# A two-layer graph and expert kernel: four up units move ahead of the routing's transposes, the routing weights of the first chunk travel alone, and two normalisations begin chunk by chunk

## What is computed

```
x = x + gnn0(layernorm(x), adj)    # attention over adj, then two GRU cells
x = x + ffn0(layernorm(x))         # one shared + 8 routed experts, hidden 512, gelu
x = x + gnn1(layernorm(x), adj)    # relu(adj @ (bilinear features) + ...)
x = x + ffn1(layernorm(x))         # 8 routed experts, hidden 256, relu

# both ffn: logits = h @ Wr (+ bias); the two largest of 8 get softmax weights, the rest 0
# out = sum over experts e of weight[:, e] * (act(h @ W1[e] + b1[e]) @ W2[e] + b2[e])
```

## Time and profile before

| | |
|---|---|
| time, three runs | 2235.76 us median (2234.46 to 2236.96) |
| time of the profiled execution | 2233.43 us, span 2231.6 us |
| busy: PE, DVE, ACT, POOL | 1819.9, 1693.7, 1398.4, 188.7 us |
| mean granted clock of PE | 0.904 of full speed |
| GRU part, its last PE work ends | 1180.0 us |
| first normalisation | 1191.9 to 1221.4 us |
| expert stage 0, from the router to the last expert | 1220.1 to 1626.9 us |
| third normalisation | 1970.1 to 1999.7 us |
| expert stage 1 | 1998.4 us to the end |

### The profile page before, as it was taken

One profiled execution on the slowest core, in us unless ns is written; L12 is line 12 of the kernel. 1 busy time (PEld: TensorE's weight loads), 2 busy tenths in 40 slices (PEclk: granted clock), 3 DMA queues, 4 the chain that ended last, 5 costly groups with the idle time before them and its releaser, 6 DMA issues.

```text
span 2231.6 us, 30437 instructions
## 1 busy us (share of the span) xinstructions
PE 1819.9 (82%) x8958; PEld 871.5 (39%) x9101; DVE 1693.7 (76%) x1792; ACT 1398.4 (63%) x1767; POOL 188.7 (8%) x154
## 2 busy tenths in 40 slices
PE   4221573899999999999797799999986699986997
PEld 4111221344444444444345344444452244462332
DVE  4555327788898888889466788888859988846998
ACT  1676006788788788788234567676645577625886
POOL 0000001100000000000442000000017700000000
PEclk7555788899999999999897899999979999977999
DMA  5997025555555554554500311221030089713542
GB/s 160 430 427 312 0 79 209 166 153 160 157 153 156 166 153 149 169 154 155 208 0 0 78 38 38 60 54 38 1 133 0 0 348 428 314 38 78 96 92 76
DMA packets 79540, 313.86 MB, mean 141 GB/s; under 512 B 13942, under 2 KB 14422, under 8 KB 69462
## 3 DMA queue, kind: packets, MB, share of 16 engines
q1 hardware_dynamic: 79468, 312.98, 41.7%
HBM read 297.88 MB, written 15.08 MB: 140 GB/s over the span
## 4 chain that ended last, share of the span: by engine, by line
PE 40%; DVE 10%; POOL 3%; issue 3%; ACT 1%; DMA 1%; DVEq 0%; SPq 0%; POOLq 0%; ACTq 0%; another core or an unknown queue 0%
PE psum L925 8%; PE psum L915 8%; PE psum L988 7%; PE psum L859 7%; POOL halves L484 3%; DVE hidp L1363 2%; DVE xT L1385 2%; DVE yT L1382 2%; DVE prod L1422 2%; PE psum L883 1%; PE psum L885 1%; PE psum L726 1%; PE psum L731 1%; PE psum L897 1%; PE psum L737 1%
## 5 line engine op out<-in xcount | busy, mean ns | idle before, releaser
L586 ACT ACTIVATE ss<-KR,dpt 128x1024 bf16<-128x1024 int16 x384 | 413.1, 1138 | 112.0 <-DVE pl L1255 111.3
L859 PE MATMUL psum<-ph,Tt 128*128 128x512 bf16 x1502 | 412.2, 381 | 8.8 <-DVE pl L1255 7.0
L669 ACT ACTIVATE hid<-psum,fB 128x512 f32<-128x512 f32 x416 | 270.7, 686 | 143.7 <-PE psum L915 89.0
L925 PE MATMUL psum<-hidp,fW 128*128 128x512 bf16 x1218 | 291.7, 381 | 28.6 <-DVE hidp L1363 22.6
L915 PE MATMUL psum<-hTp,fW 128*128 (+1 forms) x1229 | 291.3, 381 | 4.5 <-ACT mk L654 3.2
L1363 DVE TENSOR_TENSOR hidp<-hid,hidp 128x512 bf16<-128x512 f32 x416 | 268.7, 687 | 25.9 <-DVE xT L1385 10.1
L1252 DVE TENSOR_TENSOR ph<-ss,Ahi 128x3072 bf16<-128x3072 bf16 x128 | 225.2, 1759 | 62.0 <-PE psum L859 60.3
L859 PE MATMUL psum<-pl,Tt 128*128 128x512 bf16 x752 | 226.0, 381 | 0.8
L859 PEld LDWEIGHTS psum<-ph,Tt 128*128 128x128 bf16 x1536 | 150.3, 98 | 190.6 <-issue 6.4
L1255 DVE TENSOR_TENSOR pl<-ss,Alo 128x3072 bf16<-128x3072 bf16 x128 | 224.1, 1751 | 0.0
L925 PEld LDWEIGHTS psum<-hidp,fW 128*128 128x128 bf16 x1248 | 117.4, 98 | 190.2 <-issue 49.9
(11 more groups left out here) (228 smaller groups left out, 2111.0 us busy)
## 6 DMA issues: line engine op xcount, KB each, us to landing
Ar<-in_adjT SPq DMA_DIRECT2D x32, 2048.0 KB, 12.9
Ab<-in_adjT SPq DMA_DIRECT2D x128, 512.0 KB, 4.2
A<-in_adjT SPq DMA_DIRECT2D x32, 2048.0 KB, 10.4
Tt<-T_d SPq DMA_DIRECT2D x128, 256.0 KB, 2.6
mB<-mk_d SPq DMA_DIRECT2D x128, 256.0 KB, 8.0
T_d<-tb SPq DMA_DIRECT2D x32, 256.0 KB, 2.0
RD<-rden_d SPq DMA_DIRECT2D x12, 512.0 KB, 5.4
fWs<-in_W SPq DMA_DIRECT2D x2, 2304.0 KB, 16.8
```

The lines of the kernel that those rows point to most:

```text
L586: last = nc.scalar.activation(ss[s % 2][:, h, :], KR[:, h, rb * RB:(rb + 1) * RB], ACT.Sigmoid, scale=STEP, bias=dpt[:, ds(t * HEADS + h, 1)])
L669: nc.scalar.activation(hid[j % HB][:, :], psum[:, j % HB, :], func, bias=fB1[:, j:j + 1]).then_inc(act_done[k], 1)
L859: last = nc.tensor.matmul(psum[:, 2 * h + q, :], Tt[s % AS][:, h, w, :], mv[:, q * CH:(q + 1) * CH], start=fresh and k == 0, stop=False, s ...
L925: last = nc.tensor.matmul(psum[:, HB + e % dn, :], fW[1][x][:, j * P:(j + 1) * P], hidp[j % ring][:, y, :], start=(f == 0 and w == 0), sto ...
```

## The change

Nothing in the arithmetic changes. There are four edits.

1. **Stage prologue.** DVE makes `hTp[1]` ahead of the routing, not behind it. PE issues the `lag` up steps (four units, 12 matmuls) as soon as DVE has read the router's result out of bank 0, and only then waits for the routing weights. ACT works off these four units (`hidden`) ahead of the `Exp`. The transposes go to banks 4 to 7 in two rounds, the second behind ACT's copies. ACT's loop over chunks is turned by four units.
2. **Routing weights.** SP stores the first 1024 columns of `mk8` as soon as ACT has copied them, and loads chunk 0; then it stores the rest, waits for chunk 0's loads, and loads chunk 1.
3. **Normalisation 0** waits by chunk for `g_used` (and for the two halves of PSUM that the GRU part leaves); ACT's wait goes; `sqT2` and `sqT3` move to memory that POOL no longer reads.
4. **Normalisation 2** waits by chunk for `l_add`.

```diff
-        sqT = [sb(f"sqT{i}", [P, CH], F32, 48 + 2 * i) for i in range(4)]
+        sqT = [sb(f"sqT{i}", [P, CH], F32, kb) for i, kb in enumerate((48, 50, 120, 122))]
...
-                sp.wait_ge(r_mk8, 4 * k + 4)
-                sp.dma_start(mk_d[k], mk8[:, :]).then_inc(r_out, 16)
-                sp.wait_ge(r_out, 16 * (k + 1))
+                sp.wait_ge(r_mk8, 4 * k + 1)
+                sp.dma_start(mk_d[k][:, 0:2 * CH], mk8[:, 0:2 * CH]).then_inc(r_out, 16)
+                sp.wait_ge(r_out, 32 * k + 16)
...
                 weights(0, 0)
+                sp.wait_ge(r_mk8, 4 * k + 4)
+                sp.dma_start(mk_d[k][:, 2 * CH:], mk8[:, 2 * CH:]).then_inc(r_out, 16)
+                sp.wait_ge(r_out, 32 * k + 32)
+                sp.wait_ge(mB_in[k][0], 16 * NE)
                 weights(1, 1)
...
+                for j in range(HB):
+                    hidden(0, j)
+                act.wait_ge(r_sel, 3 * k + 2)
+                nc.scalar.activation(rs[:, 3, :], rs[:, 2, :], ACT.Exp).then_inc(r_exp, 1)
+                for b in range(4):
+                    act.wait_ge(r_tr, 4 * k + b + 1)
+                    half = N // 2 + b % 2 * (N // 4)
+                    nc.scalar.activation(mk8[:, b * N // 4:(b + 1) * N // 4], flat[0:NE, half:half + N // 4],
+                                         ACT.Copy).then_inc(r_mk8, 1)
+                with act.Fori(0, NC - 1) as q:
+                    for j in range(HB, nE * nF):
+                        hidden(q, j)
+                    for j in range(HB):
+                        hidden(q + 1, j)
+                for j in range(HB, nE * nF):
+                    hidden(NC - 1, j)
...
-            act.wait_ge(g_used, 2 * NC + 2)
...
+                if k == 0:
+                    pe.wait_ge(g_nin, 2 * NC + (1 if q < 4 else 2))
+                    pe.wait_ge(g_used, 2 * q + 4)
+                if k == 2:
+                    pe.wait_ge(l_add, q + 1)
...
+                pe.wait_ge(r_sel, 3 * k + 1)
                 for e in range(lag):
                     up(0, e)
+                pe.wait_ge(r_sel, 3 * k + 3)
+                for t in range(NT):
+                    if t in (16, 24):
+                        pe.wait_ge(r_mk8, 4 * k + t // 8 - 1)
+                    last = nc.tensor.transpose(flat[0:NE, N // 2 + t % 16 * P:N // 2 + t % 16 * P + P],
+                                               s1[:, t, :], ident)
+                    if t % 8 == 7:
+                        last.then_inc(r_tr, 1)
+                pe.wait_ge(r_mk8, 4 * k + 4)
...
-            pe.wait_ge(g_used, 2 * NC + 2)
...
-            pe.wait_ge(l_add, NC)
...
+                for q in range(NC):
+                    c_q = slice(q * CH, (q + 1) * CH)
+                    dve.wait_ge(fh_hi, NC * k + q + 1)
+                    V.tensor_tensor(hTp[1][:, c_q], hT[:, c_q], hTp[0][:, c_q], ALU.subtract).then_inc(f_lo, 1)
...
-                c.link(V.tensor_tensor(lg[:, :, :], ps, rb2[:, 0, :].unsqueeze(1).to_broadcast(T), ALU.add))
+                V.tensor_tensor(lg[:, :, :], ps, rb2[:, 0, :].unsqueeze(1).to_broadcast(T), ALU.add).then_inc(r_sel, 1)
```

More of the change, by code:

```diff
@@ L380, in ffn_loads @@
                     sp.dma_start(tile, src).then_inc(r_in, 16)
-                sp.wait_ge(r_mk8, 4 * k + 4)
-                sp.dma_start(mk_d[k], mk8[:, :]).then_inc(r_out, 16)
-                sp.wait_ge(r_out, 16 * (k + 1))
-                first = nE - NE
+                sp.wait_ge(r_mk8, 4 * k + 1)
+                sp.dma_start(mk_d[k][:, 0:2 * CH], mk8[:, 0:2 * CH]).then_inc(r_out, 16)
+                sp.wait_ge(r_out, 32 * k + 16)
                 def weights(s, q):
@@ L648, in ffn_scalar @@
                                          ACT.Copy).then_inc(fh_hi, 1)
[L650 to L655, removed]
                 act.sem_inc(act_done[k], HB)
@@ L663, in high, with hidden @@
                                          ACT.Copy).then_inc(hid_hi[k], 1)
[L665 to L674, removed]
+                def hidden(q, j):
+                    act.wait_ge(hid_lo[k], q * (nE * nF) + j + 1)
+                    act.wait_ge(up_done[k], q * (nE * nF) + j + 1)
+                    nc.scalar.activation(hid[j % HB][:, :], psum[:, j % HB, :], func,
+                                         bias=fB1[:, j:j + 1]).then_inc(act_done[k], 1)
+                    if j % 2:
+                        high(q, j - 1)
+                        if k == 1:
+                            high(q, j)
+                for j in range(HB):
[14 more added lines that the diff above has]
+                    hidden(NC - 1, j)
             ffn_weights(0, *FFN0)
-            act.wait_ge(g_used, 2 * NC + 2)
             lt_scalar(act, 0)
@@ L899, in ffn_tensor @@
                 last.then_inc(r_ps, 1)
[L900 to L905, removed]
                 pe.sem_inc(down_done[k], ring // nF)
@@ L1312, in ffn_vector @@
             def ffn_vector(k, nE, nF):
+                fsem, per = (dve_ffn0, dve_ffn1)[k], 2 * NE + (nE - NE)
                 dn = (3, 4)[k]
+                credits, hold, ring, lag = dn, (3, 4)[k], (12, 8)[k], (1, 2)[k]
                 T = [P, NT, NE]
+                dve.sem_inc(y_used[k], credits)
+                dve.sem_inc(hid_lo[k], HB)
+                for q in range(NC):
+                    c_q = slice(q * CH, (q + 1) * CH)
+                    dve.wait_ge(fh_hi, NC * k + q + 1)
+                    V.tensor_tensor(hTp[1][:, c_q], hT[:, c_q], hTp[0][:, c_q], ALU.subtract).then_inc(f_lo, 1)
                 dve.wait_ge(r_ps, k + 1)
                 ps = psum[:, 0, 0:NT * NE].rearrange("p (t e) -> p t e", e=NE)
-                c.link(V.tensor_tensor(lg[:, :, :], ps, rb2[:, 0, :].unsqueeze(1).to_broadcast(T), ALU.add))
+                V.tensor_tensor(lg[:, :, :], ps, rb2[:, 0, :].unsqueeze(1).to_broadcast(T), ALU.add).then_inc(r_sel, 1)
+                dve.wait_ge(r_sel, 3 * k + 1)
                 c.link(V.tensor_tensor(lg[:, :, :], lg[:, :, :], rb2[:, 1, :].unsqueeze(1).to_broadcast(T), ALU.add))
@@ L1338, in ffn_vector @@
                 V.tensor_tensor(s1[:, :, :], s1[:, :, :], s2[:, :, :], ALU.add).then_inc(r_sel, 1)
[L1340 to L1348, removed]
                 def high(q, e):
```

## The result

The changed kernel takes 2214.32 us (median of 4 runs, 2213.39 to 2218.72). The kernel before took 2235.11 us in the same comparison (4 runs, 2232.58 to 2236.96). The ratio is 0.9915, 95% interval 0.9898 to 0.9932: faster by 0.7 to 1.0%.

What follows compares the result with a forecast made beforehand. Chains of waits were taken to bind: mostly PE's in the normalisations and stage 0's prologue, DMA in stage 1's. Gains 7.6 + 2.2 + 7.9 + 3.9 = 21.6 us off 2233.43 gave 2211.8, median 2214; range 2206 to 2222.

Steps and rivals of the forecast that it cites:

- Norm 0: First normalisation: means 0 to 6 run early, chunk 7's mean and the sums at half clock; gain 7.6 us, low end 5.
- the third rival: PE at full clock in chunk 7's mean and the up units: gain 26.9 us, 9.5 in the first normalisation; 2209 us; 13%.
- Prologue 0: Stage 0, router's end to first down step: up units go first, `Exp` and transposes later; gain 2.2 us, low end 0.8.
- Norm 2: Third normalisation: PE starts at the first add and means run at full clock; gain 7.9 us, bounds 5.8 and 8.3.
- Prologue 1: Stage 1, router's end to chunk 0's weights landing: earlier, shorter store, loads alone; gain 3.9 us, bounds 1.3 and 5.7.
- From the first down step the stage runs in PE's steps as before: Body of stage 0: its length stays unchanged, so the prologue's gain is kept; 0 us of its own.
- The switch on ACT costs twice the load: Rival, ACT in both prologues: switching tables costs 2.6 us, both `Exp`s 1.3 us later; sum 19.0, time 2216.8; 15%.
- The prologues give nothing: Rival, both prologues: up units save no bounding time and `Exp` falls behind; only normalisations gain, 15.5 us, time 2220; 15%.
- PE finds its clock: Rival, first normalisation and up units: PE runs chunk 7's mean and the up units at full clock; 26.9 us, 2209; 13%.
- The turned loop stalls: Rival, ACT's loop over chunks: stalls exposed at 14 turns cost 26.8 us, making the kernel slower, 2241 us; 3%.

Runs made afterwards that it cites:

- e1: Kernel before with only the first normalisation's waits split by chunk: 2230.73 us against 2233.05, ratio 0.9987.
- c0: The changed kernel measured and profiled a second time, nothing altered: 2214.22 us, ratio 0.9912.
- e6: Changed kernel plus six extra means of chunk 6 on PE while it waits for POOL before chunk 7's mean: 2211.11 us, ratio 0.9898.
- e8: Changed kernel with both the extra means of e6 and the moved `Exp` of e7: 2207.43 us, ratio 0.9883.
- e2: Kernel before with only the third normalisation's waits split by chunk: 2227.76 us, ratio 0.9971.
- e10: Changed kernel without SP's wait for chunk 0's loads before chunk 1's: 2214.64 us, ratio 0.9913.
- e4: Kernel before with only the routing weights' store split and chunk 0 loaded alone: 2227.96 us, ratio 0.9970.
- e5: Kernel before with only the stage prologue reordered (up units and `hTp[1]` moved), `mk8` stored whole: 2238.52 us, ratio 1.0023.
- e7: Changed kernel with ACT's `Exp` between the second and third unit, and in stage 1 an unused `Exp` ahead of them: 2210.77 us, ratio 0.9897.
- e11: Kernel before with only ACT's loop over chunks turned by four units: 2230.72 us, ratio 0.9986.
- e9: e8 plus two 128x512 matmuls of zeros behind each of the last seven groups of sums, all three normalisations: 2218.15 us, ratio 0.9932.

## Why the prediction came out

**Norm 0, forecast 7.6, measured 2.2 (2.9 in time by e1, 5.4 in c0's profile): the step was mis-sized, in four of five profiles below its own low end of 5.** Its structure held: means 0 to 6 at once, chunk 7 alone at half clock (2.04 us, estimate 1.7). Two numbers failed. "I take half clock throughout: 1191.87 + 1.7 + 64 x 0.182" puts a sum at 0.182 us; 64 took 13.65, or 0.21 each, so the sums cost 2 us more. The 0.182 is 2 us shared among the 11 matmuls that the earlier trace rows counts there, but the count takes in those that only reach into the window. A window of the changed kernel shows the same 11, in the middle of its 64 in 13.65 us:

```profile
1200.00:1202.00 2.00, 2.00 (x11) 2.00 (x11) 2.00 (x1) 0.97 (x1) 0.00 (x0) 0.50 0.00 0
```

And the half clock was priced for the sums alone. The transposes and router behind were only in the low end, with 2.6 us; they took 17.5 us against 14.3, 3.2 more. These 3.2 us are the less certain part, since c0 doesn't show them; the 2 us stand in both profiles. In the kernel before, eight means in a row stood ahead of the sums, which began at full clock; one mean by itself after 5.97 us of idle time didn't raise it. e6 and e8 show the cause: with the idle time filled, the stretch is 28.1 and 28.0 us, 9.0 under before and near the 9.5 that the third rival gives PE at full clock.

**Prologue 0, forecast 2.2, measured 1.9.** Transposes at R+10.9 (forecast 10.8), first down step at R+21.1 (20.9). DVE's `hTp[1]` lies in idle time, of which 5.09 us are left ahead of the routing by DVE's timeline (7.50 before):

```profile
1225.06 0.42 DVE L1345 TENSOR_TENSOR lg<-psum,rb 128x256 f32<-128x256 f32 x1 [5.09 <-PE psum L914]
```

**Norm 2, forecast 7.9, measured 7.0 (6.5 in time by e2).** Full clock through the means as argued, 7.13 us. The forecast's own terms give 8.2 and not 7.9: 1972.7 + 3.4 = 1976.1, from 1984.27. The 3.4 us for the half of the sums that the last square waits for were too few; the chain shows 4.18, which with means that end 0.3 us later is the difference:

```profile
1962.06 4.18 PE psum L748 x32
```

**Prologue 1, forecast 3.9, measured 2.7.** Transposes at R+11.4 as forecast, the store 1.79 us (2.0). The term is off by the loads: 15.0 were taken, with bounds of 14.4 and 15.9, and they took 16.3, from the store's landing at 2005.42 (2003.63 + 1.79) to 2021.7. That "chunk 1 does not compete" bought nothing: with chunk 1's loads issued right behind them they took 15.9 before. What sets their length no run shows. The wait that keeps chunk 1 back is itself worth nothing (e10). And e4 against e5 shows what the sum of the two edits hides: the split alone gives 6.0 us here, and with the up units ahead of the `Exp` `mB` arrives 2.7 us later. e7 has both.

**What the sum left out: 2.6 us in the body of stage 0.** "From the first down step the stage runs in PE's steps as before" failed, to the good. It is the turned loop of ACT, which stood in the prediction only as the rival that makes the kernel slower; e11 shows the opposite sign. The earlier trace rows had DVE's stall of 3.83 us, but not that ACT's table load cost DVE 1.57 us just ahead of it. Also left out was that edit 1 without edit 2 is a loss (e5): the forecast said that PE, ahead by three down banks, goes on through the wait for `mB`, which holds for 2.36 us and not for 6.55.

**So the total was right by compensation.** By the first profile the sum of 21.6 us stood 5.4 us too high in norm 0, 0.3, 0.9 and 1.2 too high in the others, and lacked the body's 2.6 and -0.8 in the body of stage 1 (189.5 to 189.8 us in the kernels with edit 2, 189.1 in those without); so the edits give 15.6 us of the span's 19.9, and 4.2 are the variation of the unchanged pieces. By c0's profile the four terms give 18.4 us, 3.2 too few, the two bodies add 1.9, and the edits give 20.3: less was left to luck there, but the terms still fall short and an unforecast one fills in. The profiled execution was forecast at 2211.8 us and took 2213.51, the median at 2214 and came to 2214.32. That the medians agree to 0.3 us is no evidence for the terms; the pieces are, and in the first profile they put one of four outside its bounds.

**The rivals.** *The switch on ACT costs twice the load*: falls. The load takes 1.28 us and begins 0.02 us after the instruction before it ends; in e7 two stand around an `Exp` with no gap. The Trainium skill ("ScalarE: Activation LUTs", What ACT_TABLE_LOAD costs) counts 2.66 us with the drain; this trace shows 1.28 in all. *The prologues give nothing*: falls for the change as a whole, but e5 shows what it had in mind, edit 1 alone. *PE finds its clock*: falls for the change. Its part for the first normalisation comes true in e6, with busy work in the gap; its part for the up units doesn't, since its 12 matmuls take 4.06 us there, and 2.75 at full clock in the body. *The turned loop stalls*: falls, by e11.

## What to carry to other kernels

A wait that is split so that the work ahead of it runs sooner can leave the engine idle in the middle, and TensorE then does what follows at half clock: price the stretch behind the wait too, up to where the clock rises, and try cheap busy work in the gap. Take the price of an instruction from a long row of them, not from a count in a short window. When a step is moved ahead of the start of a chain of transfers, ask what the later landing meets: here the move lost 5.1 us by itself and paid only with the shorter store beside it. And when a total is met, compare the pieces before believing the terms, in more than one profile: the same kernel shows 2.2 us for one edit in the first profile and 5.4 in the second.

## What the runs showed of the hardware that was not expected

- Through the sums of single float32 columns the granted clock stayed at 0.50 although PE was busy for 10.00 of 10.00 us. In e6 it fell within the sums although these began at 1.00, and with two matmuls of zeros of 128x512 behind each eight sums it fell as well (e9).
- At 0.50 a sum costs 0.21 us (64 in 13.65, and eight in 1.71 in e9). Where the clock starts at 1.00 and falls on the way, 64 take 10.94 us (e6).
- The store of 8 rows of 1024 numbers landed in 1.79 us, and that of 8 rows of 4096 in 3.71.
- A table load of 1.28 us on ACT, which has idle time to spare over the stage, cost PE 1.2 us at each of two turns because it stood just ahead of a stall of DVE. Taken out of the loop (e11), or moved to run beside the stall (the changed kernel), it cost nothing, which is 2.5 us in stage 0's body.
- The same code ran its router at a mean granted clock of 0.64 in one profile and 0.81 in another, PE busy throughout in both.
